# A two-block network on one core: the state-space front of the next batch moved earlier by a slot, and its last products ahead of the last scan

## The reference, cut to what matters

```python
xb, zb = split(h @ in_proj_w)                  # 256 channels each
xb = silu(causal_conv4(xb) + conv_b)
dt, B, C = split(xb @ x_proj_w)                # 16, 16, 16 columns
dt = softplus(dt @ dt_proj_w + dt_proj_b)
decay = exp(dt * A);  inp = dt * B * xb        # for each of 16 states
h = decay * h + inp;  y = sum_n h_n * C_n      # scan over 512 steps
out = (y + xb * D) * silu(zb) @ out_proj_w
```

## Time and profile before

| | us |
|---|---|
| runs shown | 3716.63, 3720.63, 3727.23 |
| median | 3720.63 |
| profiled execution | 3714.65 |
| its span | 3712.8 |
| granted clock, mean | 0.921 of full |

### The profile page before, as it was taken

How to read it: one execution, slowest core, us unless ns; L and a number is a source line. 1 busy time by engine, 2 the same in 40 slices (tenths; PEclk the granted TensorE clock), 3 DMA queues, 4 the chain that set the end, 5 groups by cost and what they waited for, 6 DMA issues and landing times. The chain is left out here.

```text
span 3712.8 us, 53381 instructions
## 1 busy us (share of the span) xinstructions
PE 2960.3 (80%) x15912; PEld 2151.3 (58%) x15912; DVE 2858.9 (77%) x4814; ACT 1913.9 (52%) x4712; POOL 873.1 (24%) x590
## 2 busy tenths in 40 slices
PE   2487888888888878888888958888888888888886
PEld 1164565556555655565566626666666666666664
DVE  3999999999999999999999336666666666666664
ACT  3466667666666666676666434333333333333332
POOL 0443333333333433333333000111111111111111
PEclk6588999999899999999999989999999999999998
DMA  2000000000000000000000010000000000000000
GB/s 100 7 4 14 16 19 3 18 16 16 6 18 16 3 18 16 18 3 18 16 16 1 16 71 21 18 16 16 16 16 16 16 16 16 16 16 16 16 8 11
DMA packets 49771, 64.31 MB, mean 17 GB/s; under 512 B 3584, under 2 KB 36416, under 8 KB 49184
## 3 DMA queue, kind: packets, MB, share of 16 engines
q1 hardware_dynamic: 47392, 54.93, 4.6%
q10 hardware_dynamic: 2304, 8.46, 0.6%
HBM read 41.78 MB, written 21.60 MB: 17 GB/s over the span
## 5 line engine op out<-in xcount | busy, mean ns | idle before, releaser
L799 POOL TENSOR_TENSOR acc<-acc,zz 128x1024 f32<-128x1024 f32 x256 | 618.6, 2416 | 1003.3 <-DVE h L1113 995.8
L1113 DVE TENSOR_TENSOR_SCAN h<-dec,u 128x1024 f32<-128x1024 f32 x256 | 584.0, 2281 | 3.0
L926 PEld LDWEIGHTS bank<-one_sb,hid 128*128 128x128 f32 x4096 | 484.4, 194 | 29.8 <-DVE facc L1180 13.7
L926 PE MATMUL bank<-one_sb,hid 128*128 128x128 f32 x4096 | 486.5, 277 | 12.6 <-DVE facc L1180 12.6
L874 PE MATMUL bank<-S,pick_sb 96*128 96x512 bf16 x512 | 215.7, 427 | 286.9 <-DVE zz L1122 177.3
L621 ACT ACTIVATE dec<-dt,aneg 128x512 f32<-128x512 f32 (+1 forms) x512 | 341.8, 721 | 114.0 <-DVE h L1113 96.3
L158 POOL TENSOR_SCALAR n_ve<-n_mv 128x4 f32<-128x4 f32 x96 | 49.3, 514 | 1471.9 <-DVE n_mv L141 1471.9
L874 PEld LDWEIGHTS bank<-S,pick_sb 96*128 96x128 bf16 x512 | 51.1, 100 | 490.8 <-DVE zz L1122 264.6
L1122 DVE TENSOR_TENSOR zz<-h,bank 128x1024 f32<-128x1024 f32 x256 | 312.5, 1221 | 8.8
L1106 DVE TENSOR_TENSOR u<-dtx,bank 128x1024 f32<-128x1024 f32 x256 | 310.3, 1212 | 4.0 <-issue 3.6
L653 ACT ACTIVATE hid<-banks,one_sb 128x512 f32<-128x512 f32 x352 | 240.8, 693 | 112.4 <-PE bank L926 77.8
(11 more groups left out here) (265 smaller groups left out, 6963.1 us busy)
## 6 DMA issues: line engine op xcount, KB each, us to landing
kv_dram<-Gs ACTq DMA_DIRECT2D x16, 516.5 KB, 3.9
kvl<-kv_dram SPq DMA_DIRECT2D x16, 516.5 KB, 3.6
xs<-in_x SPq DMA_DIRECT2D x16, 256.0 KB, 2.8
x<-in_x SPq DMA_DIRECT2D x16, 256.0 KB, 2.9
x_dram<-x SPq DMA_DIRECT2D x16, 256.0 KB, 2.1
h_dram<-hT SPq DMA_DIRECT2D x16, 256.0 KB, 2.0
h<-h_dram SPq DMA_DIRECT2D x16, 256.0 KB, 2.6
x2s<-x_dram SPq DMA_DIRECT2D x16, 256.0 KB, 2.7
```

The costliest lines, as they stand in the source:

```text
L799: pool.tensor_tensor(acc[:, :, :], acc[:, :, :], zz[:, k % 2, :, :], ALU.add)\
L926: last = pe.matmul(bank1(f"down{e}")[:, j * D:(j + 1) * D], hid[:, e % 2, f, j * P:(j + 1) * P], w2[:, e, f, :], start=(f == 0), stop=(f = ...
L1113: dve.tensor_tensor_scan(h[:, :, :].rearrange("p g t -> p (g t)"), dec[:, k % 2, :, :].rearrange("p g t -> p (g t)"), u[:, :, :].rearrange ...
```

## The change

The front of n is moved one slot earlier as far as `split_mid` and `split_low` (`norm_stats` and `norm_pool` to slot 6, `norm_apply`, `turn1` and `modulate1` to slot 7, `in_x` and `keep_x` to 8 and 9, `convolve` to 9 and 10, `silu_x` to 10, `x_proj` and `split_x` to 11, `dt_proj` to 12 and 13, the magnitudes to 12 and 13, ACT's `softplus` to 14). On PE, `in_x` and `x_proj` are issued ahead of the slot's `UPS_POST` tiles and its `downs`; on ACT, `keep_x` and `split_x` are issued ahead of the relus of `UPS_POST`. DVE's `softplus` (`dt`, `dtx`) goes from the tail to slot 16, ahead of the last scan. ACT's `decay(0, n)` goes ahead of both `keep_products`.

```diff
-            XIN = {9: 0, 10: 1}
-            CONV = {10: 0, 11: 1}
+            XIN = {8: 0, 9: 1}
+            CONV = {9: 0, 10: 1}
...
@@ scalar: after the relus of UPS_PRE
+                            if n is not None:
+                                if slot in XIN:
+                                    keep_x(XIN[slot], n)
+                                if slot == 11:
+                                    split_x(n)
...
                             if n is not None:
-                                if slot == 8:
+                                if slot == 7:
                                     modulate1(n)
-                                if slot in XIN:
-                                    keep_x(XIN[slot], n)
-                                if slot == 11:
+                                if slot == 10:
                                     silu_x(n)
                                 if slot == 12:
-                                    split_x(n)
-                                if slot == 13:
                                     round_rest(n)
                                     magnitude(0, n)
+                                if slot == 13:
+                                    magnitude(1, n)
                                 if slot == 14:
-                                    magnitude(1, n)
-                                if slot == 15:
                                     softplus(n)
                         if n is not None:
                             keep_split(a, n)
+                            decay(0, n)
                         if y is not None:
                             keep_products(0, y)
-                        if n is not None:
-                            decay(0, n)
-                        if y is not None:
                             keep_products(1, y)
...
@@ gpsimd
-                            if n is not None and slot == 7:
+                            if n is not None and slot == 6:
                                 norm_pool(pool, L1, half, n, passed)
...
@@ tensor: after spread(k + 1, 0, a), ahead of the other tiles
+                            if n is not None:
+                                if slot in XIN:
+                                    in_x(XIN[slot], n, s)
+                                if slot == 11:
+                                    x_proj(n, s)
...
                             if n is not None:
-                                if slot == 8:
+                                if slot == 7:
                                     turn1(n, s)
-                                if slot in XIN:
-                                    in_x(XIN[slot], n, s)
-                                if slot == 12:
-                                    x_proj(n, s)
-                                if slot in (13, 14):
-                                    dt_proj(slot - 13, n, s)
+                                if slot in (12, 13):
+                                    dt_proj(slot - 12, n, s)
...
@@ vector
-                                if slot == 7:
+                                if slot == 6:
                                     dve.wait_ge(*x_in(n, 16))
                                     norm_stats(dve, L1, xs, n, passed)
-                                if slot == 8:
+                                if slot == 7:
...
                                     norm_apply(dve, L1, xs, n)
                                 if slot in CONV:
                                     convolve(CONV[slot], n)
+                                if slot == 12:
+                                    split_mid(n)
                                 if slot == 13:
-                                    split_mid(n)
-                                if slot == 14:
                                     split_low(n)
+                            if n is not None and slot == NS:
+                                softplus(n)
                             if a is not None and k >= 0:
                                 scans(k, a)
                                 weigh(k, a)
...
-                        if n is not None:
-                            softplus(n)
                         if b is not None:
                             take(E0 - 1, b)
```

## The result

| | before | changed |
|---|---|---|
| runs, us | 3716.63 to 3727.23 | 3868.12 to 3872.76 |
| median | 3721.63 | 3870.64 |
| profiled execution | 3714.65 | 3870.85 |
| its span | 3712.8 | 3869.0 |
| mean granted clock | 0.921 | 0.900 |

The changed kernel takes 1.0400 times as long (95% interval 1.0382 to 1.0418). It was forecast slower, at 3806 in a range from 3727 to 3875; +149 us came where +85 was forecast. The result lies only 4 us inside the upper end of the range. A step grew from 127.1 to 137.3 us (starts of `dtx`, mean of steps 3 to 14).

The account below looks back on a forecast made before the run. DVE was taken to bound the first sweep, busy 1297 of 1400 us. Per step 8.8 us of new waits against 5.55 saved, taken as 2.9, plus 3.75 for clock made 6.65; over the sweep +88, forecast 3806, range 3727 to 3875.

Parts of the forecast that it names:

- The two PE waits: Slots 8 and 10 to 12: PE held for ACT's `hT` and `xc`; DVE waits 3.2 and 5.6 us a step.
- the clock: PE at half clock behind three idle gaps: 1.5 us each, half for the first, 3.75 a step.
- What it takes away: Savings per step: `xpad` 1.75, `Sn` 2.0, key tile 1.1, `norm_apply` 0.3, `dt` with `dtx` 0.4; sum 5.55 us.
- `dt` and `dtx`: Ahead of the last scan: 3.2 us gained, 2.0 and 0.5 lost at L1188, 0.3 at `out_proj`; 0.4 a step left.
- my three gaps: PE idle 2.5 us in slot 8, 2.5 to 2.8 ahead of slot 10, 3.9 in slot 11.
- rival 2: Half clock for the whole of each slot: 12.5 us a step, about +165, 3880; chance 0.08.
- The sum: 2.9 + 3.75 = 6.65 us a step, thirteen steps 86.5; step 1 4.5, step 0 -3.2; together +88.
- The table load: In ACT's chain to `xc`: load alone, 1.3 us; with the skill's drain, `xc` 1.4 later and thirteen steps 18 more.

Follow-up runs that it names:

- e4_fill: The changed kernel with products of constants put into PE's gaps in slot 8, ahead of slot 10, ahead of `x_proj` and in the tail: 3782.57 us.
- e1_pe_behind: The changed kernel with `in_x` and `x_proj` on PE back behind the slot's expert tiles and `downs`: 3684.44 us, ratio 0.9907 against the kernel before.
- e2_dt_alone: The kernel before with only `dt` and `dtx` ahead of the last scan and the first decay ahead of the key products: 3713.0 us, ratio 0.998.
- e5_in_behind: The changed kernel with only `in_x` back behind the tiles and `downs` of slots 8 and 9, `x_proj` staying ahead: 3772.18 us.

## Why the prediction was right, and where its size was off

- **The two PE waits.** Right in place and cause. `in_x` waits 2.50 us (2.5 said); `x_proj` waits 4.65 (3.9 said), as `downs(2)` ends 1.9 us behind scan 9 and not with it. From the end of `downs(2)` to `xc` ACT's chain takes 6.5 us (6.4 said), first and last of it on the timeline of the changed kernel:

```profile
1207.06 0.69 ACT L653 ACTIVATE hid<-banks,one_sb 128x512 f32<-128x512 f32 x1 [6.86 <-PE bank L925]
...
1211.17 1.28 ACT L570 ACT_TABLE_LOAD   x1
1212.46 1.06 ACT L570 ACTIVATE xc<-cv 128x1024 f32<-128x1024 f32 x1
```

  At full clock `take(1)` and `take(3)` wait 3.30 and 6.57 in e4_fill (3.2 and 5.6 said). So the second wait was said 1.0 too short even without the clock. That a step still grew by only 3.1 at full clock (2.9 said) is in part luck; what made up for it isn't shown.
- **What it takes away.** Right: `Sn`, `xpad` and the key tile's wait went. e1_pe_behind, which keeps `Sn` at 2.1, `xpad` at 0.5 and `take` at 0.4 a step, is 37 us faster than the kernel before; by my terms it should be (5.55 - 3.0) x 13 + 3 = 36.
- **`dt` and `dtx`.** The collision moved to L1188, as read from step 15: 2.4 us back (2.5 said), 0.6 a step gained alone (0.4 said). As the Trainium skill has it ("SBUF — State Buffer", Terms), it is a lock that one of the two waits out: POOL's pair ends at 1120.82, L1188 0.4 us later.
- **The mis-sized term is the clock: 3.75 a step said, 7.1 measured** (137.3 less 130.2, the steps of the changed kernel and of e4_fill; 88 us over thirteen steps give 6.8). Set beside e4_fill place by place:
  - Slot 8, the shortest of my three gaps, which I had counted half: 0.75 said. `take(1)` waits 4.9 us in two steps of three and 6.4 in the third (in two takes), 5.4 on average, against 3.3: 2.1.
  - Slots 10 and 11: 3.0 said. `take(3)` waits 9.8 on average against 6.6: 3.3. This was nearly right.
  - The tail: nothing said. I had carried the lateness of `products` on to `out_proj` (0.3) but not asked what PE does while it waits. 1.7.
- **How near it was.** That 3870.64 lies inside the range is in part luck. It is nearer to rival 2 (3880) than to the forecast (3806). But rival 2's mechanism, half clock for the whole of each slot, isn't there: in slot 11 `x_proj` is at half clock and `downs(3)` takes its 3.73 us. What came in its place is the tail. My reading that two gaps of a step are followed by half clock was short too: the trace of the kernel before also has a granted clock of 0.50 at 1062 to 1064 and at 1072 to 1074.
- **The sum.** Measured takes 15.0 more, `out_proj` 1.7, L1188 2.4; less `Sn` 2.0, `xpad` 1.75, the key tile 1.05, `dt` and `dtx` 3.2, `norm_apply` 0.3: +10.8 a step, against 10.2 by the starts of `dtx` (6.65 said). Thirteen steps of 10.2 are 133 us of the 149. Step 1, which has no keys, grew by 11.5 where 4.5 was said, and step 0 shrank by 4.3 (3.2 said); the remaining 9 are not accounted for.
- **The table load.** The chain of 6.5 us has room for the load alone, 1.28 and nothing behind it; the Trainium skill's 2.66 for load and drain ("ScalarE: Activation LUTs", What ACT_TABLE_LOAD costs) isn't seen here.

Open: what decides whether a gap is followed by half clock. Its length alone doesn't, as the tail shows: 2.06 us and half clock in the changed kernel, 2.07 us and full clock in e2_dt_alone and e5_in_behind. The same question stands behind the two lengths of the waits of `take(3)` in the changed kernel, about 9.6 and 10.3 us.

## What to carry to other kernels

An instruction moved ahead in an in-order queue is worth its own lateness only; its wait is paid by all that stands behind it. So ask first when its input is ready, and move the wait, not the work: the same front in the same earlier slots is 1% faster behind `downs` and 4% slower ahead of it. A wait of 2 to 5 us put on PE can have a second price at the clock, here 7.1 us a step beside the 9.9 of the two waits themselves, and it falls due on whatever hangs on PE next. The collision of DVE and POOL moved with the order. Here it met L1188, which works in SBUF alone; `zz` and `take`, which read a PSUM bank, kept their 1.22 and 0.73 us beside the same additions.

## What the runs showed of the hardware

The length of a PE gap doesn't tell whether half clock follows. In the changed kernel a gap of 2.06 us was followed by a granted clock of 0.51 (1118 to 1120), and one of 3.50 us by 1.00 (1138 to 1140). In the kernel before a gap of only 1.31 us, with one of 3.48 some 8 us ahead of it, came before 0.50 (1072 to 1074). The same gap of 2.07 us in the tail was followed by 1.00 in e2_dt_alone and e5_in_behind. And products of constants in the gaps pay: they took 88 us from the changed kernel and 20 from the one before, with more for PE to do in both.
